# Edge messages of a graph network summed as two float32r parts, with the one-hot table as weights

## The reference

```python
h = jnp.concatenate([x[row], edge_attr], axis=1)   # 64 + 32 features for each edge
h = jax.nn.relu(h @ W1 + b1)                       # 128 hidden values for each edge
h = h @ W2 + b2
agg = scatter_mean(h, col, x.shape[0])             # mean over the edges that end in a node
g = jnp.concatenate([x, agg], axis=1)
g = jax.nn.relu(g @ W3 + b3)
return g @ W4 + b4
```

## Time and profile before

| | |
|---|---|
| device time, median of 3 runs | 1945.89 us (1943.58 to 1948.28) |
| span of the profiled execution, first to last instruction | 1945.2 us |
| edge network, first to last add of VectorE | 1060.0 to 1341.3 us of the span |
| busy in the whole span | PE 1270.0, PEld 1164.5, DVE 998.1, ACT 739.7, POOL 578.6 us |
| mean granted TensorE clock | 0.815 of full speed |

### The profile page before, as it was taken

How to read it: one execution, slowest core, us unless ns; L and a number is a source line. 1 busy time by engine, 2 the same in 40 slices (tenths; PEclk the granted TensorE clock), 3 DMA queues, 4 the chain that set the end, 5 groups by cost and what they waited for, 6 DMA issues and landing times.

```text
span 1945.2 us, 47461 instructions
## 1 busy us (share of the span) xinstructions
PE 1270.0 (65%) x19829; PEld 1164.5 (60%) x19830; DVE 998.1 (51%) x2349; ACT 739.7 (38%) x2012; POOL 578.6 (30%) x683
## 2 busy tenths in 40 slices
PE   5201001000002787778998999998799998998897
PEld 3200000000001666667897999998799998898897
DVE  8000002000010666674457566565788888887887
ACT  5000000000001777773213344343566666655464
POOL 2777777777772000000001444441010010000000
PEclk8555555555555999889997999998899999899999
DMA  7431000001010999997474888884766661344442
GB/s 222 141 133 35 15 15 13 14 27 38 13 54 35 357 370 379 387 369 265 174 289 175 315 308 304 301 306 170 252 247 233 224 247 56 143 168 158 175 178 92
DMA packets 86126, 359.64 MB, mean 185 GB/s; under 512 B 23740, under 2 KB 35281, under 8 KB 78929
## 3 DMA queue, kind: packets, MB, share of 16 engines
q1 hardware_dynamic: 72594, 348.83, 48.3%
q0 software_dynamic: 13312, 7.69, 1.7%
HBM read 250.77 MB, written 105.68 MB: 183 GB/s over the span
## 4 chain that ended last, share of the span: by engine, by line
PE 45%; another core or an unknown queue 21%; issue 12%; DVE 12%; ACT 7%; DMA 2%; SPq 1%; POOL 0%; ACTq 0%; DVEq 0%; POOLq 0%
PE ps L2998 8%; PE ps L3619 7%; PE ps L2650 7%; PE ps L2986 6%; PE ps L3266 5%; PE ps L3633 2%; DMA arena<-recs 2%; PE ps L2525 2%; PE ps L2510 1%; DVE arena L3208 1%; DVE arena L3209 1%; ACT arena L2570 1%; DVE arena L2389 1%; PE ps L3322 1%
## 5 line engine op out<-in xcount | busy, mean ns | idle before, releaser
L2178 POOL DMA_INDIRECT recs<-arena x416 | 423.8, 1019 | 164.9 <-issue 132.2
L3056 POOL CAST arena<-arena 128x512 f32<-128x512 bf16 (+1 forms) x175 | 119.4, 684 | 615.2 <-DMA arena<-hot_out 447.8
L3619 PE MATMUL ps<-arena 125*128 125x64 bf16 x5850 | 192.8, 194 | 10.0 <-issue 10.0
L3619 PEld LDWEIGHTS ps<-arena 125*128 125x128 bf16 x5850 | 187.7, 99 | 11.9 <-issue 11.8
L2998 PE MATMUL ps<-arena 128*128 128x125 f32 x1300 | 182.2, 282 | 0.0
L3665 ACT ACTIVATE arena<-ps,arena 128x64 f32<-128x64 f32 x650 | 141.0, 333 | 102.9 <-PE ps L3633 102.9
L2510 PE MATMUL ps<-arena 128*128 128x128 bf16 x625 | 66.9, 232 | 166.5 <-issue 157.3
L3142 DVE TENSOR_TENSOR arena<-ps,arena 128x512 f32<-128x512 f32 (+1 forms) x175 | 114.1, 653 | 118.4 <-PE ps L2986 115.4
L3089 ACT ACTIVATE arena<-arena 128x512 f32<-128x512 f32 (+1 forms) x175 | 105.0, 601 | 171.4 <-DVE arena L3142 171.4
L2570 ACT ACTIVATE arena<-ps 128x512 f32<-128x512 f32 (+1 forms) x192 | 83.8, 523 | 215.8 <-remote 183.7
L2998 PEld LDWEIGHTS ps<-arena 128*128 128x128 f32 x1300 | 158.8, 192 | 0.0
(11 more groups left out here) (385 smaller groups left out, 2414.5 us busy)
## 6 DMA issues: line engine op xcount, KB each, us to landing
arena<-ids_out SPq DMA_DIRECT2D x100, 832.0 KB, 6.2
arena<-hot_out SPq DMA_DIRECT2D x75, 832.0 KB, 6.2
arena<-e_out SPq DMA_DIRECT2D x25, 1664.0 KB, 6.9
arena<-adj_out SPq DMA_DIRECT2D x41, 800.0 KB, 6.5
e_out<-arena SPq DMA_DIRECT2D x25, 1024.0 KB
hot_out<-arena SPq DMA_DIRECT2D x25, 832.0 KB, 7.1
adj_out<-arena SPq DMA_DIRECT2D x25, 800.0 KB, 6.4
e_out<-arena SPq DMA_DIRECT2D x25, 640.0 KB
```

Source lines behind the costliest of these rows:

```text
L2178: nc.gpsimd.indirect_dma_start(out=recs, out_offset=bass.IndirectOffsetOnAxis(ap=slot_row[:, t:t + 1], axis=0), in_=rec_in[:, t, :], in_of ...
L3056: nc.gpsimd.tensor_copy(hot_e[s % NH][:, 0:len(js), :], hot_in[d % 2][:, js[0]:js[0] + len(js), :])\
L3619: ins = M(bank(step % 4, C, k * C), hot_r[d % 2][r][0:NP_, j * SLOTS:(j + 1) * SLOTS], px3[:, block_of(d, j), piece, r * C:(r + 1) * C], s ...
```

## The change

The sum over edges is turned round. The one-hot table of target nodes becomes the weights (128 columns of it), and the messages become the moving operand. Messages and table are float32r, a form of float32 that TensorE takes rounded. Each message is split in two parts: ScalarE writes the relu, rounded to float32r, into the first half of `act_two`; VectorE computes relu minus that first part into the second half (`rest`, one more 128x512 instruction in each step). The two parts stand side by side, so a tile's matmul moves 256 columns: 128 hidden features, twice. The sum comes out as node by (part, feature), in 256 columns of the bank.

At the end of a block VectorE adds the two parts out of PSUM (`both`, a reduction of 125x256 to 125x128), TensorE transposes the result back, and VectorE multiplies by the reciprocal degrees, two steps later than before (`TURN_SUM`). The node network's offsets move two steps with it. `pre` has three buffers instead of two, the float32 one-hot table four instead of eight, and a matmul of the sum waits for `act_rest` besides.

```diff
+NE = 4
...
-        act_out = [e1_at([128, 4 * HID]) for _ in range(4)]
-        hot_e = [e1_at([128, 4, 128]) for _ in range(NH)]
+        act_two = [rounded[:, k * 8 * HID:(k + 1) * 8 * HID].rearrange("p (k t h) -> p k t h", t=2, h=HID)
+                   for k in range(4)]
+        hot_e = [rounded[:, (32 + 4 * k) * HID:(36 + 4 * k) * HID].rearrange("p (k n) -> p k n", n=128)
+                 for k in range(NE)]
...
+        pre.append(e2_at([128, 4 * HID]))
...
+        TURN_SUM = 2
...
-            return 7 * (tiles(c)[-1] + 1) + LAG + 2
+            return 7 * (tiles(c)[-1] + 1) + LAG + TURN_SUM + 2
...
                     pe.wait_ge(sem("act_relued"), s + 1)
+                    pe.wait_ge(sem("act_rest"), s + 1)
                     for k, j in enumerate(groups(d)[g]):
-                        ins = M(bank(4 + d % 2, NP_), act_out[s % 4][:, k * HID:(k + 1) * HID],
-                                hot_e[s % NH][:, k, 0:NP_], start=j == 0, stop=j == NT, skip_group_check=True)
+                        ins = M(bank(4 + d % 2, 2 * HID), hot_e[s % NE][:, k, :],
+                                act_two[s % 4][:, k, :, :].rearrange("p t h -> p (t h)"), start=j == 0, stop=j == NT,
+                                skip_group_check=True)
                     ins.then_inc(sem("act_summed"), 1)
+                d, at = divmod(step - LAG - TURN_SUM, 7)
+                if at == 0 and 1 <= d <= NT:
+                    d -= 1
+                    pe.wait_ge(sem("both_added"), d + 1)
+                    nc.tensor.transpose(bank(4 + d % 2, NP_, 2 * HID), both[d % 2], ident[0:NP_, 0:NP_])\
+                        .then_inc(sem("sum_turned"), 1)
...
+            def rest(s):
+                n = len(groups(s // 7)[s % 7])
+                dve.wait_ge(sem("act_relued"), s + 1)
+                if s >= 4:
+                    dve.wait_ge(sem("act_summed"), s - 3)
+                V.scalar_tensor_tensor(out=act_two[s % 4][:, 0:n, 1, :],
+                                       in0=pre[s % 3][:, 0:n * HID].rearrange("p (k h) -> p k h", h=HID), scalar=0.0,
+                                       in1=act_two[s % 4][:, 0:n, 0, :].bitcast(F32), op0=ALU.max, op1=ALU.subtract)\
+                    .then_inc(sem("act_rest"), 1)
...
+                if 1 <= step <= G7:
+                    rest(step - 1)
...
+                    got = bank(4 + d % 2, 2 * HID)[0:NP_, :]
+                    V.tensor_reduce(both[d % 2], got.rearrange("p (t h) -> p h t", t=2), AX, ALU.add).then_inc(sem("both_added"), 1)
+                d, at = divmod(step - LAG - TURN_SUM - 1, 7)
+                if at == 0 and 1 <= d <= NT:
+                    d -= 1
+                    dve.wait_ge(sem("sum_turned"), d + 1)
```

More of the change, by code:

```diff
@@ L11 @@
 F16 = mybir.dt.float16
+F32R = mybir.dt.float32r
 U16 = mybir.dt.uint16
@@ L45 @@
 NH = 8
+NE = 4
+LOW_AT = 9464
+ROUNDED = 6144
 SLOTS = 128
@@ L212, in build @@
         ps = ctx.enter_context(nc.psum_tensor("ps", [128, 8 * BANK], F32))
-        arena = sb("arena", [128, ARENA])
         iota_i = sb("iota_i", [128, 128], I32)
@@ L222, in build @@
         flag = sb("flag", [1, 1], I32)
+        with nc.sbuf_tensor("arena", [128, ARENA], F32) as arena:
+            pass
+        sb("below", [128, LOW_AT])
+        rounded = sb("rounded", [128, ROUNDED], F32R)
         keep = Carver(arena)
@@ L278, in build @@
         px = e1_at([NP_, NT, PIECES, HID], BF16)
-        act_out = [e1_at([128, 4 * HID]) for _ in range(4)]
         hot_in = [e1_at([128, SB, 128], BF16) for _ in range(2)]
-        hot_e = [e1_at([128, 4, 128]) for _ in range(NH)]
+        assert e1_at.at == LOW_AT
+        act_two = [rounded[:, k * 8 * HID:(k + 1) * 8 * HID].rearrange("p (k t h) -> p k t h", t=2, h=HID)
+                   for k in range(4)]
+        hot_e = [rounded[:, (32 + 4 * k) * HID:(36 + 4 * k) * HID].rearrange("p (k n) -> p k n", n=128)
+                 for k in range(NE)]
+        e1_at.at += ROUNDED
         assert e1_at.at <= rest_at
@@ L295, in build @@
         low_end, high_end = e1_at.at, e2_at.at
+        pre.append(e2_at([128, 4 * HID]))
+        both = [y1[0:NP_, (11 + k) * HID:(12 + k) * HID] for k in range(2)]
         ln1_sq = y1[0:NP_, 0:13 * C].rearrange("p (i f) -> p i f", f=C)
@@ L2891, in hid_step @@
         def hid_step(c):
-            return 7 * (tiles(c)[-1] + 1) + LAG + 2
+            return 7 * (tiles(c)[-1] + 1) + LAG + TURN_SUM + 2
         OUT, EVICT, ROOT, SCALED, TURN, TURNED, HUP, HIGH, LEFT, MID, LOW = 3, 4, 9, 11, 13, 15, 17, 19, 21, 23, 25
-        E_STEPS = 7 * (NT + 1) + LAG + 2 + LOW + 1
+        E_STEPS = 7 * (NT + 1) + LAG + TURN_SUM + 2 + LOW + 1
         def started(step, off):
@@ L3053, in pool_edge2 @@
                     pool.wait_ge(sem(f"hot_back{d % 2}"), hot_landed(d, 0))
-                if s >= NH:
-                    pool.wait_ge(sem("act_summed"), s - NH + 1)
-                nc.gpsimd.tensor_copy(hot_e[s % NH][:, 0:len(js), :], hot_in[d % 2][:, js[0]:js[0] + len(js), :])\
+                if s >= NE:
+                    pool.wait_ge(sem("act_summed"), s - NE + 1)
+                nc.gpsimd.tensor_copy(hot_e[s % NE][:, 0:len(js), :], hot_in[d % 2][:, js[0]:js[0] + len(js), :])\
                     .then_inc(sem("dst_hot"), 1)
@@ L3088, in act_edge2 @@
                         act.wait_ge(sem("act_summed"), step - 3)
-                    A(act_out[step % 4][:, 0:m], pre[step % 2][:, 0:m], ACT.Relu).then_inc(sem("act_relued"), 1)
+                    A(act_two[step % 4][:, 0:m // HID, 0, :], pre[step % 3][:, 0:m].rearrange("p (k h) -> p k h", h=HID),
+                      ACT.Relu).then_inc(sem("act_relued"), 1)
                 for c in range(NCH):
@@ L3139, in dve_edge2 @@
                     dve.wait_ge(sem("px_got"), step + 1)
-                    if step >= 2:
-                        dve.wait_ge(sem("act_relued"), step - 1)
-                    V.tensor_tensor(pre[step % 2][:, 0:m], bank(step % 4, m),
+                    if step >= 3:
+                        dve.wait_ge(sem("act_rest"), step - 2)
+                    V.tensor_tensor(pre[step % 3][:, 0:m], bank(step % 4, m),
                                     e1_in[d % 2][:, 4 * g * HID:4 * g * HID + m], ALU.add).then_inc(sem("e1_added"), 1)
+                if 1 <= step <= G7:
+                    rest(step - 1)
                 if step < G7 and d + 1 < NT:
@@ L3154, in dve_edge2 @@
                     dve.wait_ge(sem("act_summed"), 7 * d + 7)
+                    if d >= 2:
+                        dve.wait_ge(sem("sum_turned"), d - 1)
+                    got = bank(4 + d % 2, 2 * HID)[0:NP_, :]
[4 more added lines that the diff above has]
+                    dve.wait_ge(sem("sum_turned"), d + 1)
                     c, k = divmod(d, CH)
@@ L3157, in dve_edge2 @@
                         dve.wait_ge(sem(f"rcp_in{c % 2}"), 16 * (c // 2 + 1))
-                    V.tensor_tensor(agg[:, d * NP_:(d + 1) * NP_], bank(4 + d % 2, NP_),
+                    V.tensor_tensor(agg[:, d * NP_:(d + 1) * NP_], bank(4 + d % 2, NP_, 2 * HID),
                                     rcp_row[c % 2][:, k * NP_:(k + 1) * NP_], ALU.mult).then_inc(sem("agg_read"), 1)
```

## The result

The changed kernel takes 1953.1 us (median of 20 runs, 1950.3 to 1960.5), the kernel before 1947.8 (median of 20, 1943.6 to 1957.1): a ratio of 1.0026, 95% interval 1.0015 to 1.0037. It is slower by about 5 us, small but clear of the noise.

The account below looks back on a forecast made before the run. TensorE alone was taken to pace the 281.3 us stretch. Afterwards VectorE's 258.5 us of work plus 28.7 of waits make 287.2, +5.9; with 1.0 at the end +6.9, so 1953 us, range 1930 to 1976.

Parts of the forecast that it names:

- VectorE takes over: First to last add: VectorE becomes the bound with 258.5 us of work, TensorE needs 208; this case has chance 0.50.
- The port: GpSimd's casts and VectorE instructions with two SBUF inputs exclude each other; losses 7.2, 6.0, 1.5 and 5.0 us.
- The place of the remainders' loss: At a block's reduction and multiplication a cast goes first and holds the remainder: 0.30 us each block, 7.2 in all.
- the slower rival: Casts go ahead of remainders in half of the 175 steps, holding each about 0.3 us: 1973 us; chance 0.15.
- The wait behind the node network: VectorE waits 1.8 us before an add behind the node network's two matmuls, five times: 9.0 us.
- The plain step: In plain steps the next remainder starts ahead of the cast, which runs beside the following add: no loss.
- The sum's matmul: On TensorE, a float32r matmul with 256 columns takes 0.11 us if it streams like bf16; a sum 0.45 us.
- TensorE's limit for being hidden: TensorE's need in the stretch stays under 281 us up to 0.22 us a tile for the sum.
- Four float32 tables instead of eight: Casts are released four steps before they are needed, 4 x 1.3 us, and take 0.61 us: cost nothing.
- VectorE's bare work: What VectorE must do between first and last add with nothing waiting: 258.5 us, 22 of it the chunks' work.
- The end: At the stretch's end the last block's reduction, transpose and two more handovers lie open: 1.0 us.

Follow-up runs that it names:

- rest_short: Changed kernel with the remainder made for one tile of four from the fifth step on, 128 wide instead of 512: 1912.9 us, ratio 0.9814.
- cast_act: Changed kernel with the casts of the one-hot table on ScalarE instead of GpSimd: 1934.1 us, ratio 0.9921.
- bf16_parts: Changed kernel with both operands of the sum in bf16 instead of float32r: 1947.6 us, one execution.
- before_rest: Kernel before with only the remainder on VectorE added, written over pre and used by nobody, the sum still float32: 1956.6 us, ratio 1.0049.
- hid_late: Changed kernel with the node network's two matmuls and all that hangs on them two steps later: 1962.2 us, ratio 1.0074.
- one_part: Changed kernel with only the first part of the messages summed, 128 float32r columns moving instead of 256: 1965.8 us, one execution.

## Why the prediction was right

The forecast was +6.9 us, VectorE the bound; measured +5.3 between the medians. What takes over and what VectorE loses were right in kind and in sum; where it loses was partly wrong.

- VectorE takes over, TensorE drops well below it: shown by the trace (270.8 and 235.7 of 282.8 us) and by rest_short and cast_act, where less work or less loss on VectorE shortened the stretch.
- The port: 7.2 + 6.0 + 1.5 + 5.0 = 19.7 us forecast, 17 measured, and shown by cast_act. The parts fell otherwise than I had them. Comparisons lost 25 x 0.25 = 6.3 us where I had put half of 10: 18 of the 25 took 1.43 us. Remainders lost 9.3, the layer norm and the bias add 1.3.
- The place of the remainders' loss was wrong. I had it behind a block's reduction and multiplication, and gave remainders of about 1.0 us there as a sign; in all blocks those have their plain length. The loss of a block stands behind the half add instead (ten at 1.08, nine at 0.76, some 5 us in all), where the slower rival had TensorE late, behind the transpose. That the sum came near is in part luck.
- The wait behind the node network: 5 x 1.8 = 9.0 us forecast, 5 x 1.78 = 8.9 measured, with the cause as laid out; the other 3 us of VectorE's idle time, in part waits for gathers in the first steps, I had at nothing. What I wouldn't have forecast is that moving it later makes things worse.
- The plain step is free: remainders 0.68 us, with the cast held up and not VectorE.
- The sum's matmul: 0.11 us forecast, 0.147 measured. From the start of a sum to that of the gathers behind it, TensorE takes 0.56 us a step instead of 0.45. I had priced it like bf16, for which bf16_parts does give 0.11. It cost nothing here, since TensorE's limit for being hidden was 0.22.
- Four float32 tables instead of eight, at nothing: the profile puts 21.1 us of the weight loads' waits down to casts, in 20 places. TensorE isn't the bound, and rest_short ran at 242.6 us with the same four, so it set no pace here.
- VectorE's bare work was too large: 258.5 us, against the 253.8 that it is busy in cast_act's stretch, where nothing collides. Adds and remainders follow each other at 0.60 instead of 0.605, which is 1.5 us, and most of the rest is the chunk's work, which I had as what other numbers left over.
- The end: +1.0 forecast, +2.1 measured. The last block's last sum starts 3.6 us after the last add's end instead of 2.9, because the last remainder now stands behind two comparisons of the attention on VectorE (in the timeline it starts at 1348.99, the add it belongs to had ended at 1345.99), which I had not read from the order; and from that add to the last multiplication it is 6.0 us instead of 4.3.

So in the profiled pair the stretch came out at +1.5 instead of +5.9 us. The losses are as forecast, 17 + 11.9 = 29 us against 28.7, and the difference is the bare work, 4.7 us too large; the end came out at +2.1 instead of +1.0. The total of +6.9 lies nearer to the medians' +5.3 than to the pair's own +3.6, and that nearness is luck within the drift of single executions.

## What to carry to other kernels

A cheaper instruction on the engine that sets the pace is worth only the distance to the next engine, and what is moved to that engine must be counted at its spacing, waits included. Before VectorE is given an instruction with two SBUF inputs in every step, look who else uses that port: here moving GpSimd's casts to ScalarE was worth 17 us with the remainder and nothing without it. And where two engines each need about 95% of a stretch or more, expect it to be longer than either's work: before_rest had VectorE and TensorE busy 95 and 98% of 289.1 us, and both waited, where TensorE alone had set 281.2.

## What I had not expected of the hardware

- A float32r matmul with 128 weight columns costs 0.147 us a piece with 256 columns moving and still 0.12 with 128, where bf16 with 256 costs 0.11; its weight load is listed as long as float32's, 0.19 us.
- The granted clock differed between orders of much the same work: 0.91 to 0.98 in hid_late from 1100 us on, with TensorE busy 80 to 88% of each piece, and 0.90 in one_part, busy 86%, against 1.00 in the changed kernel, busy 80 to 87%. The share of busy time in the profile doesn't tell them apart.
- VectorE does not keep the port from one instruction to the next: a comparison right behind a remainder lost 0.35 us in 18 of 25 blocks (1.43 instead of 1.08), with a cast waiting or just begun, so the cast goes in between even though VectorE's next instruction is ready.
